# The six projections of half the tokens, issued over four steps of cross-attention instead of three

## The chip, the cores and the metric

The kernel runs on one core of a Trainium2 chip. The metric is the device time of one execution in microseconds (us): median 1030.58 of three runs, 1029.69 to 1031.92.

The engines are named as the profile names them: PE is TensorE (matmuls and transposes), PEld its weight load, DVE is VectorE, ACT is ScalarE, POOL is GpSimd, SP is the queue that issues most DMAs. They run side by side, each in its own order of instructions, and wait for one another through semaphores.

## What is computed

One decoder layer on 8 sequences of 128 tokens, 512 wide, in 32-bit floats: self-attention, cross-attention with a context of the same size, and a feed-forward part, each on a layer norm of its input and added to it. The change lies in the cross-attention alone:

```python
q = (query @ Wq).reshape(nb, q_len, H, D).transpose(0, 2, 1, 3)     # H = 32 heads, D = 128
k = (key @ Wk).reshape(nb, q_len, KVH, D).transpose(0, 2, 1, 3)     # KVH = 8
v = (value @ Wv).reshape(nb, q_len, KVH, D).transpose(0, 2, 1, 3)
q = q * cos + _rotate_half(q) * sin
k = k * cos + _rotate_half(k) * sin
...
scores = jnp.einsum('bhqd,bhkd->bhqk', q, k) / jnp.sqrt(jnp.float32(D))
scores = jnp.where(mask == 0, jnp.float32(-1000000000.0), scores)
attn = jax.nn.softmax(scores, axis=-1)
x = jnp.einsum('bhqk,bhkd->bhqd', attn, v)
x = x.transpose(0, 2, 1, 3).reshape(nb, q_len, H * D)
return x @ Wo
```

## The kernel before

Cross-attention runs over 8 groups `g`; a group is one key head with its four query heads. A group has 8 steps `b`, one for each sequence. Step `b` issues on PE, in this order:

- the scores of sequence `b` (line 1030, four small matmuls into SC, bank 2 or 3);
- projections and output products, as two tables say. `blocks_in(b)` lists projections as (piece `j`, half of the tokens, group ahead). Pieces are 0 = keys, 1 to 4 = the four query heads, 5 = values; they are called K, q0, q1, q2, q3 and V below. Each is 12 matmuls (line 624, called by `project`) into PB, bank 0 for even `j` and bank 1 for odd `j`. Steps 0 to 3 serve half 1 of this group, steps 4 to 7 half 0 of the next. `outputs_in(b)` lists output products O(y), also 12 matmuls of line 624, all into YB, bank 7: O(-3), O(-2), O(-1) (sequences 5 to 7 of the group before) in steps 0, 1 and 2, none in step 3, O(0) in step 4, O(1) and O(2) in step 5, O(3) in step 6, O(4) in step 7. The order in a step is: first projection, outputs named `before`, second projection, outputs named `after`;
- the product of probabilities and values of sequence `b - 2` (called pv here, three matmuls of line 624 into OB, bank 6);
- the transposes of the probabilities of sequence `b - 1` (line 1060, into TB, bank 4 or 5);
- in the step that has V, four transposes of the values (`transpose_v`, line 998).

The other engines follow the same steps. For each piece but V, DVE applies the rotation with three operations (`rope`, lines 838 to 840) and POOL adds the two parts (`rope_sum`, line 798). V goes another way: ACT copies the projected bank to SBUF (`v_copy`, line 919, tile `rotated`), PE transposes it back into the same bank, ACT and DVE take high and low part (`v_high`, line 925; `v_low`, line 844). In a step DVE first masks the scores (line 873) and takes their negated maximum (line 876), then comes to the ropes and the additions of outputs to `x` (`add_output`, line 852), then to the reciprocal of the row sums (line 895) and two low parts (lines 898, 901). ACT first takes the four exponentials of the step (line 938), then `v_copy` where the step has V, then two copies (lines 948, 953), `v_high`, and casts of weights (line 610), whose low parts POOL takes (line 618). POOL in a step comes to the rope sums, then to the normalisation of the probabilities (line 813), then to the weights.

Three waits matter to what follows. All output products share one bank, so each one waits for the addition of the one before it (this is the wait on `x2`); the transposes of the values wait for `v_copy`, which stands behind the step's exponentials:

```python
    pe.wait_ge(sem["x2"], SEQS * g + y)          # in output(g, y)
    pe.wait_ge(sem["vT"], 2 * g + half + 1)      # in transpose_v(g, half)
    pe.wait_ge(sem["probsT_low"], n - 1)         # ahead of the pv product
```

The first group has no outputs in its steps 0 to 2; the last one has no projections in steps 4 to 7 and orders its outputs differently from step 5 on.

Of the kernel before, what the change touches and what calls it, by code (L numbers as in the profile page):

```python
# [581 lines left out]
PIECES = 6  # L582
# [51 lines left out]
def norm_stats(nc, dve, m, sem, k):  # L634
    if k >= EARLY:
        dve.wait_ge(sem["x2"], SEQS * (GROUPS - 1) + NORM_SEQ[k] + 1)
    if k > 0:
        dve.wait_ge(sem["norm_mv"], k)
    nc.vector.bn_stats(m["norm_stats"][:], m["x"][:, NORM_SEQ[k], :]).then_inc(sem["norm_stats"], 1)  # L639
    dve.wait_ge(sem["norm_stats"], k + 1)  # L640
    nc.vector.bn_aggr(m["norm_mv"][:, k, :], m["norm_stats"][:]).then_inc(sem["norm_mv"], 1)  # L641
# [57 lines left out]
def half_of(t, half):  # L699
    return t[..., half * HT:(half + 1) * HT]  # L700


def cross_attention(nc, m, sem, ps, io):
# [7 lines left out]
    with ExitStack() as stack:  # L711
# [18 lines left out]
        def norm_bank(k):  # L730

            return PB[k % 2] if k >= EARLY else (SC[1], YB)[k]

        def rows_of(k):
            return m["norm_rows"][:, k % 2, :] if k >= EARLY else last_hs[:, k, :]
# [6 lines left out]
        def norms_in(table, b, last, tail):  # L742
            return table.get(SEQS + b if tail else b, []) if last else []

        def blocks_in(b):

            pairs = {0: (0, 1), 1: (2, 3), 2: (4, 5)}
            return [(j, 1, 0) for j in pairs.get(b, ())] + [(j, 0, 1) for j in pairs.get(b - 4, ())]

        def turns_in(b, last):  # L750
# [23 lines left out]
        @block.sync  # L774
        def _(sp):
            def body(g, last):
                for b in range(SEQS):
                    for which, ahead, t in turns_in(b, last):
                        if which < PIECES:
                            source = piece_source(io, which, g + 1)  # L780
                        else:
                            source = io["wo2"][bass.ds((g * QUAD + which - PIECES) * P, P), :]
                        load_piece(sp, m, sem, PIECES + TURNS * g + t, (PIECES + t) % SLOTS, source)

            with sp.Fori(0, GROUPS - 1) as g:
                body(g, False)
            body(GROUPS - 1, True)
            sp.wait_ge(sem["piece_split"], PIECES + TURNS * (GROUPS - 1) + QUAD)
            load_ff_rows(sp, m, sem, io, 0)
# [37 lines left out]
        @block.vector  # L827
        def _(dve):
            def rope(g, half, j, first=False):

                rr = 10 * g + 5 * half + j
                pb = PB[j % 2]
                dve.wait_ge(sem["projected"], 12 * g + 6 * half + j + 1)
                if not first and j == 0:
                    dve.wait_ge(sem["v_transposed"], 2 * g + half)
                if not first or j >= 2:
                    dve.wait_ge(sem["roped"], rr - 1)
                nc.vector.tensor_tensor(rot[:, (half + j) % 2, :], pb[:], half_of(m["cosT"][:], half), ALU.mult)  # L838
                nc.vector.tensor_tensor(cross[0:64, (half + j) % 2, :], pb[64:128, :], half_of(m["sinT"][0:64, :], half), ALU.mult)
                nc.vector.tensor_tensor(cross[64:128, (half + j) % 2, :], pb[0:64, :], half_of(m["sinT"][64:128, :], half), ALU.mult).then_inc(sem["rope_read"], 1)  # L840

            def v_low(g, half):
                dve.wait_ge(sem["v_high"], 2 * g + half + 1)
                nc.vector.tensor_tensor(v[:, 1, half * HALF:(half + 1) * HALF, :], PB[1][:].rearrange("p (b d) -> p b d", b=HALF),
                                        v[:, 0, half * HALF:(half + 1) * HALF, :].bitcast(F32), ALU.subtract).then_inc(sem["v_low"], 1)

            def add_output(g, y, first):

                dve.wait_ge(sem["out2"], SEQS * g + y + 1)
                if not (first and y == 0):  # L850
                    dve.wait_ge(sem["x2"], SEQS * g + y)
                nc.vector.tensor_tensor(x[:, y % SEQS, :], x[:, y % SEQS, :], YB[:], ALU.add).then_inc(sem["x2"], 1)  # L852

            for k in range(EARLY):
                norm_stats(nc, dve, m, sem, k)
            for k in range(EARLY):
                norm_rows(nc, dve, m, sem, k, rows_of(k))
            for j in range(PIECES - 1):
                rope(0, 0, j, first=True)
                if j < EARLY:  # L860
                    norm_low(nc, dve, m, sem, j, norm_bank(j))
            v_low(0, 0)

            def body(g, first, last, tail=False):
                for b in range(3 if tail else SEQS):
                    n = SEQS * g + b
                    blocks = [x for x in blocks_in(b) if not (x[2] and last)] if not tail else []
                    if not tail:

                        dve.wait_ge(sem["scores2"], n + 1)  # L870
                        if not first or b >= 2:
                            dve.wait_ge(sem["probs_transposed2"], n - 1)
                        nc.vector.scalar_tensor_tensor(out=S[:, b % 2], in0=SC[b % 2][:].rearrange("p (h k) -> p h k", h=QUAD), scalar=SCALE2,
                                                       in1=cap[:, b, :].unsqueeze(1).to_broadcast([P, QUAD, P]), op0=ALU.mult, op1=ALU.min).then_inc(sem["masked2"], 1)
                        dve.wait_ge(sem["masked2"], n + 1)
                        nc.vector.tensor_reduce(negmax[:, b % 2, :], S[:, b % 2], AX.X, ALU.max, negate=True).then_inc(sem["max2"], 1)  # L876
                    for j, half, ahead in blocks[:1]:
                        rope(g + ahead, half, j)
                    before, after, late = outputs_in(b, first, last, tail)
                    for y in before:  # L880
                        add_output(g, y, first)
                    for j, half, ahead in blocks[1:]:
                        if j < PIECES - 1:
                            rope(g + ahead, half, j)
                    for y in after:
                        add_output(g, y, first)
                    for k in norms_in(NORM_LOWS, b, last, tail):
                        norm_low(nc, dve, m, sem, k, norm_bank(k))
                    for k in norms_in(NORM_STATS, b, last, tail):
                        norm_stats(nc, dve, m, sem, k)  # L890
                    for k in norms_in(NORM_ROWS, b, last, tail):
                        norm_rows(nc, dve, m, sem, k, rows_of(k))
                    if not tail:
                        dve.wait_ge(sem["exp2"], n + 1)
                        nc.vector.reciprocal(rinv[:, b % 2, :], rowsum[:, b % 2, :]).then_inc(sem["rinv2"], 1)  # L895
                    if (not first or b >= 2) and (not tail or b < 2):
                        dve.wait_ge(sem["outT_high"], n - 1)
                        nc.vector.tensor_tensor(oT[:, b % 2, 1], OB[:], oT[:, b % 2, 0].bitcast(F32), ALU.subtract).then_inc(sem["outT_low"], 1)  # L898
                    if (not first or b >= 1) and (not tail or b < 1):
                        dve.wait_ge(sem["probsT_high"], n)  # L900
                        nc.vector.tensor_tensor(PT[:, 1], TB[(b - 1) % 2][:], PT[:, 0].bitcast(F32), ALU.subtract).then_inc(sem["probsT_low"], 1)
                    for j, half, ahead in blocks[1:]:
                        if j == PIECES - 1:
                            v_low(g + ahead, half)
                    for y in late:
                        add_output(g, y, first)

            body(0, True, False)
            with dve.Fori(1, GROUPS - 1) as g:
                body(g, False, False)  # L910
            body(GROUPS - 1, False, True)
            body(GROUPS, False, True, tail=True)

# [63 lines left out]
        def _(pe):  # L977
# [42 lines left out]
            def body(g, first, last, tail=False):  # L1020
                for b in range(3 if tail else SEQS):
                    n = SEQS * g + b
                    blocks = [x for x in blocks_in(b) if not (x[2] and last)] if not tail else []
# [30 lines left out]
                    if (not first or b >= 1) and (not tail or b < 1):  # L1054
# [4 lines left out]
                        for h in range(QUAD):  # L1059
                            i = nc.tensor.transpose(TB[(b - 1) % 2][:, h * P:(h + 1) * P], S[:, (b - 1) % 2, h, :], ident[:])  # L1060
                        i.then_inc(sem["probs_transposed2"], 1)
                    for j, half, ahead in blocks[1:]:
                        if j == PIECES - 1:
                            transpose_v(g + ahead, half)
                    for y in late:
# [300 lines left out]
```

## Time and profile before

| what | value |
|---|---|
| time, median of three runs | 1030.58 us (1029.69 to 1031.92) |
| profiled execution: span from first to last instruction | 1029.7 us |
| PE busy (matmuls) | 1003.1 us, 97% |
| DVE busy | 581.3 us, 56% |
| ACT busy | 428.1 us, 42% |
| POOL busy | 381.6 us, 37% |
| mean granted TensorE clock over the span | 0.992 of full |

No time of its own is shown for the profiled execution beside its span; the span is 0.9 us below the median of the runs. The cross-attention fills the stretch from about 236 to 828 us. Matmuls overlap, so the start of one row to the start of the next is what a row takes of PE's time, and the busy time of a row is a little more than that.

### The profile page before, as it was taken

Reading aid. Unit: us, or ns where it says so; the run is one execution under the profiler, and the core shown is the slowest. Engines: PE = TensorE matmul, PEld = TensorE weight load, DVE = VectorE, ACT = ScalarE, POOL = GpSimd, SP = SyncE. Lnnn points to the kernel's source line nnn. Section 1 sums busy time; section 2 is a strip of 40 time slices with the busy share of each in tenths; the row PEclk is TensorE's granted clock in tenths of the full one; section 3 lists DMA queues with packets and bytes.
Section 4 is the critical chain, followed back from the end, with each engine's and each line's share of the span. In section 5 each row is a group of like instructions: output and inputs, shape, how many; then the busy total and the mean of one; then the engine's idle time right before and its main releaser. Section 6 shows DMA issues by size and latency. Waiting matters only on the chain. (4 is left out here: it accounts for less than half of the span.)

```text
span 1029.7 us, 16071 instructions
## 1 busy us (share of the span) xinstructions
PE 1003.1 (97%) x5260; PEld 822.9 (80%) x5260; DVE 581.3 (56%) x973; ACT 428.1 (42%) x1239; POOL 381.6 (37%) x375
## 2 busy tenths in 40 slices
PE   5999999989999999999999999999999999999998
PEld 3787777876888888888888888888887778888787
DVE  3765555636776666767666666766765852222101
ACT  2777666751533433533533434434334433332100
POOL 7422222253642642643634534626424222222100
PEclk8999999989999999999999999999999999999999
DMA  6000000211110210210210201201100022221001
GB/s 199 12 11 11 11 10 10 62 52 52 50 54 1 73 32 0 71 31 0 74 27 20 72 10 31 61 10 49 43 1 32 1 62 61 61 69 47 11 31 41
DMA packets 45699, 39.98 MB, mean 39 GB/s; under 512 B 3617, under 2 KB 34465, under 8 KB 45665
## 3 DMA queue, kind: packets, MB, share of 16 engines
q1 hardware_dynamic: 45280, 38.48, 12.7%
q0 software_dynamic: 384, 1.05, 0.3%
q8 instruction: 20, 0.33, 0.1%
q14 instruction: 15, 0.11, 0.0%
HBM read 37.43 MB, written 2.10 MB: 38 GB/s over the span
## 5 line engine op out<-in xcount | busy, mean ns | idle before, releaser
L624 PE MATMUL bank<-cross_wo_hl,cross_outT_hl 128*128 128x512 f32 x768 | 191.7, 398 | 1.0 <-POOL cross_wo_hl L618 0.6
L624 PE MATMUL bank<-hsT_hl,cross_wqkv_hl 128*128 128x512 f32 x768 | 188.2, 394 | 0.0
L624 PEld LDWEIGHTS bank<-cross_wo_hl,cross_outT_hl 128*128 128x128 f32 x768 | 143.1, 188 | 35.5 <-POOL cross_wo_hl L618 1.6
L624 PEld LDWEIGHTS bank<-hsT_hl,cross_wqkv_hl 128*128 128x128 f32 x768 | 141.9, 188 | 29.3
L938 ACT ACTIVATE cross_scores<-cross_scores,cross_negmax 128x128 f32<-128x128 f32 x256 | 99.8, 391 | 127.1 <-DVE cross_negmax L876 127.1
L798 POOL TENSOR_TENSOR cross_qT<-rotated,rotated_other_half 128x512 f32<-128x512 f32 x64 | 82.8, 1293 | 162.0 <-DVE rotated_other_half L840 162.0
L624 PE MATMUL bank<-hsT_hl,ff_gate_upT_hl 128*128 128x512 f32 (+1 forms) x528 | 126.3, 395 | 0.5 <-DVE ff_gate_upT_hl L1140 0.5
L624 PEld LDWEIGHTS bank<-hsT_hl,ff_gate_upT_hl 128*128 128x128 f32 (+1 forms) x528 | 96.3, 186 | 21.9 <-DVE ff_gate_upT_hl L1140 0.8
L948 ACT CAST cross_outT_hl<-bank 128x512 fp32r<-128x512 f32 x64 | 37.1, 579 | 143.4 <-PE bank L624 142.5
L838 DVE TENSOR_TENSOR rotated<-bank,cosT 128x512 f32<-128x512 f32 x80 | 55.2, 690 | 71.4 <-PE bank L624 71.2
L624 PE MATMUL bank<-ctxT_hl,cross_wqkv_hl 128*128 128x512 f32 x384 | 94.3, 394 | 1.1 <-PEq L74 1.1
L813 POOL TENSOR_TENSOR cross_scores<-cross_scores,cross_rinv 128x512 f32<-128x512 f32 x64 | 66.6, 1041 | 67.1 <-DVE cross_rinv L895 65.8
L399 ACT ACTIVATE self_probs<-self_scores,self_negmax 128x128 f32<-128x128 f32 x256 | 81.8, 393 | 20.8 <-DVE self_negmax L293 20.8
L624 PEld LDWEIGHTS bank<-ctxT_hl,cross_wqkv_hl 128*128 128x128 f32 x384 | 71.0, 188 | 16.4 <-issue 1.9
L898 DVE TENSOR_TENSOR cross_outT_hl<-bank,cross_outT_hl 128x512 fp32r<-128x512 f32 x64 | 43.5, 679 | 56.3 <-ACT cross_outT_hl L948 56.3
L290 DVE TENSOR_TENSOR self_scores<-bank,alibi_bias 128x512 f32<-128x512 f32 x64 | 44.0, 688 | 44.9 <-PE bank L498 44.5
L1127 POOL TENSOR_TENSOR ff_hT_hl<-ff_work,ff_hT_hl 128x512 f32 (+2 forms) x22 | 28.4, 1292 | 107.1 <-ACT ff_hT_hl L1202 107.1
L1030 PE MATMUL bank<-cross_kT,cross_qT 128*128 128x128 f32 x512 | 67.6, 275 | 0.0
L518 PEld LDWEIGHTS bank<-self_v_and_ones,self_probsT 128*128 128x128 f32 x512 | 63.8, 196 | 2.7 <-ACT self_probsT L384 2.6
L518 PE MATMUL bank<-self_v_and_ones,self_probsT 128*128 (+1 forms) x512 | 63.5, 257 | 2.2 <-ACT self_probsT L384 2.2
L852 DVE TENSOR_TENSOR x<-x,bank 128x512 f32<-128x512 f32 x64 | 44.0, 687 | 34.9 <-PE bank L624 34.7
L1030 PEld LDWEIGHTS bank<-cross_kT,cross_qT 128*128 128x128 f32 x512 | 62.4, 192 | 0.2
(121 smaller groups left out, 1565.7 us busy)
## 6 DMA issues: line engine op xcount, KB each, us to landing
staged_rows<-in_wq SPq DMA_DIRECT2D x32, 256.0 KB, 2.8
staged_rows<-in_wo SPq DMA_DIRECT2D x32, 256.0 KB, 2.7
staged_rows<-in_wg SPq DMA_DIRECT2D x10, 256.0 KB, 2.6
staged_rows<-in_wu SPq DMA_DIRECT2D x10, 256.0 KB, 2.8
staged_rows<-in_wd SPq DMA_DIRECT2D x10, 256.0 KB, 3.0
ctx_tok<-in_ctx SPq DMA_DIRECT2D x8, 256.0 KB, 2.6
staged_rows<-in_wk SPq DMA_DIRECT2D x8, 256.0 KB, 3.1
staged_rows<-in_wv SPq DMA_DIRECT2D x8, 256.0 KB, 3.1
```

The source lines that it names most:

```text
L290: nc.vector.tensor_tensor(S[:, s % 2], SC[s % 2][:].rearrange("p (h k) -> p h k", h=QUAD), bias[:, QUAD * s:QUAD * s + QUAD, :], ALU.add). ...
L399: e = nc.scalar.activation(PR[:, s % 2, j, :], S[:, s % 2, j, :], ACT.Exp, bias=negmax[:, s % 2, j:j + 1])
L518: i = nc.tensor.matmul(OB[r // HALF][:, c:c + HD1 + 1], PT[:, r % 2, j, :], v[:, bass.ds(owner, 1), :].rearrange("p b d -> p (b d)"), star ...
L624: i = nc.tensor.matmul(out, stationary[:, a], moving[:, b], start=(first and k == 0), stop=(last and k == 2))
L798: nc.gpsimd.tensor_tensor(half_of(dst, half), rot[:, (half + j) % 2, :], cross[:, (half + j) % 2, :], ALU.add).then_inc(sem["roped"], 1)
L813: nc.gpsimd.tensor_tensor(S[:, b % 2], S[:, b % 2], rinv[:, b % 2, :].unsqueeze(2).to_broadcast([P, QUAD, P]), ALU.mult).then_inc(sem["pro ...
L838: nc.vector.tensor_tensor(rot[:, (half + j) % 2, :], pb[:], half_of(m["cosT"][:], half), ALU.mult)
L852: nc.vector.tensor_tensor(x[:, y % SEQS, :], x[:, y % SEQS, :], YB[:], ALU.add).then_inc(sem["x2"], 1)
L898: nc.vector.tensor_tensor(oT[:, b % 2, 1], OB[:], oT[:, b % 2, 0].bitcast(F32), ALU.subtract).then_inc(sem["outT_low"], 1)
L938: e = nc.scalar.activation(S[:, b % 2, h, :], S[:, b % 2, h, :], ACT.Exp, bias=negmax[:, b % 2, h:h + 1], accum_out=rowsum[:, b % 2, h:h + 1])
L948: nc.scalar.copy(oT[:, b % 2, 0], OB[:]).then_inc(sem["outT_high"], 1)
L1030: i = nc.tensor.matmul(SC[b % 2][:, h * P:(h + 1) * P], qT[:, h, b * P:(b + 1) * P], kT[:, b * P:(b + 1) * P], start=True, stop=True)
```

## The change

The table of projections is spread over four steps instead of three. V stands alone in step 3 (and 7), q1 alone in step 1 (and 5), q2 and q3 in step 2 (and 6). The other edits let a step whose only projection is V go through `v_low` and `transpose_v` and not through `rope`; ACT and POOL read the same table.

```diff
-            pairs = {0: (0, 1), 1: (2, 3), 2: (4, 5)}
+            pairs = {0: (0, 1), 1: (2,), 2: (3, 4), 3: (5,)}
             return [(j, 1, 0) for j in pairs.get(b, ())] + [(j, 0, 1) for j in pairs.get(b - 4, ())]
...
                     for j, half, ahead in blocks[:1]:
-                        rope(g + ahead, half, j)
+                        if j < PIECES - 1:
+                            rope(g + ahead, half, j)
...
-                    for j, half, ahead in blocks[1:]:
+                    for j, half, ahead in blocks:
                         if j == PIECES - 1:
                             v_low(g + ahead, half)
...
-                    for j, half, ahead in blocks[1:]:
+                    for j, half, ahead in blocks:
                         if j == PIECES - 1:
                             transpose_v(g + ahead, half)
```

PE, end of step 2, step 3 and start of step 4 of a middle group, before. The products from `ctxT_hl` are V (bank 1) and K (bank 0) of this place, bank 6 is pv, line 1060 transposes probabilities, line 998 the values, line 1030 makes scores:

```order
L624 MATMUL bank1<-ctxT_hl,cross_wqkv_hl 128x512 x12
L624 MATMUL bank6<-cross_probsT_hl,cross_v_hl 128x512 x3
L1056 REGISTER_ALU
L1060 MATMUL bank5<-ident,cross_scores 128x128 x4
L996 REGISTER_ALU
L998 MATMUL bank1<-ident,rotated 128x128 x4
L1030 MATMUL bank3<-cross_kT,cross_qT 128x128 x4
L624 MATMUL bank6<-cross_probsT_hl,cross_v_hl 128x512 x3
L1056 REGISTER_ALU
L1060 MATMUL bank4<-ident,cross_scores 128x128 x4
L1026 REGISTER_ALU
L1030 MATMUL bank2<-cross_kT,cross_qT 128x128 x4
```

The same place of the changed kernel, whose lines here are one higher:

```order
L624 MATMUL bank0<-hsT_hl,cross_wqkv_hl 128x512 x12
L624 MATMUL bank6<-cross_probsT_hl,cross_v_hl 128x512 x3
L1057 REGISTER_ALU
L1061 MATMUL bank5<-ident,cross_scores 128x128 x4
L1031 MATMUL bank3<-cross_kT,cross_qT 128x128 x4
L987 REGISTER_ALU
L624 MATMUL bank1<-ctxT_hl,cross_wqkv_hl 128x512 x12
L624 MATMUL bank6<-cross_probsT_hl,cross_v_hl 128x512 x3
L1057 REGISTER_ALU
L1061 MATMUL bank4<-ident,cross_scores 128x128 x4
L997 REGISTER_ALU
L999 MATMUL bank1<-ident,rotated 128x128 x4
```

V has moved from step 2 into step 3, between the scores and the pv product; its transposes come at the end of step 3; step 2 now ends with q3 from `hsT_hl`.

ACT, step 2 of a middle group, before (line 938 are the exponentials, line 919 is `v_copy`, lines 948 and 953 the two copies, line 925 `v_high`):

```order
L938 ACTIVATE cross_scores,cross_rowsum<-cross_scores,cross_negmax 128x128 x4
L917 REGISTER_ALU
L918 ISA
L919 COPY rotated<-bank1 128x512
L948 CAST cross_outT_hl<-bank6 128x512
L953 CAST cross_probsT_hl<-bank5 128x512
L925 CAST cross_v_hl<-bank1 128x512
```

ACT, step 3 of a middle group, after:

```order
L939 ACTIVATE cross_scores,cross_rowsum<-cross_scores,cross_negmax 128x128 x4
L918 REGISTER_ALU
L919 ISA
L920 COPY rotated<-bank1 128x512
L949 CAST cross_outT_hl<-bank6 128x512
L954 CAST cross_probsT_hl<-bank4 128x512
L926 CAST cross_v_hl<-bank1 128x512
```

The copy of V keeps its place behind the exponentials of its step, but that is now step 3.

PE, step 5 of a middle group, before, from the scores to pv (bank 7 holds the output products, banks 0 and 1 the projections q1 and q2):

```order
L1030 MATMUL bank3<-cross_kT,cross_qT 128x128 x4
L986 REGISTER_ALU
L624 MATMUL bank0<-hsT_hl,cross_wqkv_hl 128x512 x12
L624 MATMUL bank7<-cross_wo_hl,cross_outT_hl 128x512 x12
L986 REGISTER_ALU
L989 REGISTER_ALU
L624 MATMUL bank1<-hsT_hl,cross_wqkv_hl 128x512 x12
L624 MATMUL bank7<-cross_wo_hl,cross_outT_hl 128x512 x12
L624 MATMUL bank6<-cross_probsT_hl,cross_v_hl 128x512 x3
```

And after:

```order
L1031 MATMUL bank3<-cross_kT,cross_qT 128x128 x4
L987 REGISTER_ALU
L624 MATMUL bank0<-hsT_hl,cross_wqkv_hl 128x512 x12
L624 MATMUL bank7<-cross_wo_hl,cross_outT_hl 128x512 x24
L624 MATMUL bank6<-cross_probsT_hl,cross_v_hl 128x512 x3
```

q2 has left step 5 for step 6; O(1) and O(2) stand side by side, both in bank 7.

## Rows read from the trace of the kernel before

**Rows 1.** The page: busy time, share of the span, instructions.

```profile
PE 1003.1 (97%) x5260; PEld 822.9 (80%) x5260; DVE 581.3 (56%) x973; ACT 428.1 (42%) x1239; POOL 381.6 (37%) x375
```

**Rows 2.** PE's waits: for whom, us in total, times, longest.

```profile
PE bank L624 <- DVE cross_probsT_hl L901: 2.2, 9, 0.3
```

**Rows 3.** Timeline of PE, middle group, step 1's products to step 4: start, length.

```profile
411.70 1.06 PE L1030 MATMUL bank<-cross_kT,cross_qT 128*128 128x128 f32 x8
412.51 3.01 PE L624 MATMUL bank<-hsT_hl,cross_wqkv_hl 128*128 128x512 f32 x12
415.36 2.97 PE L624 MATMUL bank<-cross_wo_hl,cross_outT_hl 128*128 128x512 f32 x12
418.17 2.89 PE L624 MATMUL bank<-ctxT_hl,cross_wqkv_hl 128*128 128x512 f32 x12
420.90 0.86 PE L624 MATMUL bank<-cross_probsT_hl,cross_v_hl 128*128 128x512 f32 x3
421.60 0.60 PE L1060 MATMUL bank<-ident,cross_scores 128*128 128x128 f32 x4
422.03 0.60 PE L998 MATMUL bank<-ident,rotated 128*128 128x128 f32 x4
422.47 1.06 PE L1030 MATMUL bank<-cross_kT,cross_qT 128*128 128x128 f32 x8
423.76 0.97 PE L624 MATMUL bank<-cross_probsT_hl,cross_v_hl 128*128 128x512 f32 x3 [0.23 <-DVE cross_probsT_hl L901]
424.57 0.60 PE L1060 MATMUL bank<-ident,cross_scores 128*128 128x128 f32 x4
425.00 1.06 PE L1030 MATMUL bank<-cross_kT,cross_qT 128*128 128x128 f32 x8
```

**Rows 4.** Timeline of the same group, one group on: the same scores.

```profile
498.01 1.06 PE L1030 MATMUL bank<-cross_kT,cross_qT 128*128 128x128 f32 x8
```

**Rows 5.** Timeline of DVE and ACT around the scores of 411.70.

```profile
410.85 0.69 DVE L838 TENSOR_TENSOR rotated<-bank,cosT 128x512 f32<-128x512 f32 x1 [2.13 <-PE bank L624]
414.25 0.68 DVE L873 SCALAR_TENSOR_TENSOR cross_scores<-bank,cap 128x512 f32<-128x512 f32 x1
414.29 1.03 POOL L813 TENSOR_TENSOR cross_scores<-cross_scores,cross_rinv 128x512 f32<-128x512 f32 x1
415.68 0.40 ACT L938 ACTIVATE cross_scores<-cross_scores,cross_negmax 128x128 f32<-128x128 f32 x1 [1.51 <-DVE cross_negmax L876]
417.15 0.18 ACT L938 ACTIVATION_READ_ACCUMULATOR cross_scores<-cross_scores,cross_negmax 128x1 f32 x1
```

**Rows 6.** Timeline of the opening of cross-attention: copy and transposes of V.

```profile
253.94 0.58 ACT L919 COPY rotated<-bank 128x512 f32<-128x512 f32 x1 [10.32 <-PE bank L624]
254.58 0.66 PE L998 MATMUL bank<-ident,rotated 128*128 128x128 f32 x4 [0.68 <-ACT rotated L919]
255.07 1.06 PE L1030 MATMUL bank<-cross_kT,cross_qT 128*128 128x128 f32 x8
```

**Rows 7.** Timeline of DVE: the addition of the output product of 415.36.

```profile
418.37 0.69 DVE L852 TENSOR_TENSOR x<-x,bank 128x512 f32<-128x512 f32 x1 [0.63 <-PE bank L624]
```

**Rows 8.** Timeline of the first group: scores of step 1, POOL's probabilities of step 0.

```profile
261.44 1.05 PE L1030 MATMUL bank<-cross_kT,cross_qT 128*128 128x128 f32 x8
265.06 1.03 POOL L813 TENSOR_TENSOR cross_scores<-cross_scores,cross_rinv 128x512 f32<-128x512 f32 x1
```

**Rows 9.** Timeline of the last group, step 4: weights on POOL, O(0) and pv.

```profile
789.01 5.02 POOL L618 TENSOR_TENSOR cross_wo_hl<-staged_rows,cross_wo_hl 128x512 fp32r<-128x512 f32 x4 [3.69 <-ACT cross_wo_hl L610]
790.88 1.70 PE L624 MATMUL bank<-cross_wo_hl,cross_outT_hl 128*128 128x512 f32 x6
794.89 0.86 PE L624 MATMUL bank<-cross_probsT_hl,cross_v_hl 128*128 128x512 f32 x3
```

**Rows 10.** Stretches: length, then busy time (instructions) of the engines, granted clock, DMA.

```profile
216.00:220.00 4.00, 2.78 (x13) 1.54 (x12) 1.99 (x5) 0.76 (x3) 4.00 (x4) 1.00 0.34 98
224.00:228.00 4.00, 3.10 (x15) 3.02 (x16) 0.68 (x2) 0.00 (x0) 0.00 (x0) 0.50 0.00 0
824.00:828.00 4.00, 3.11 (x13) 2.18 (x12) 1.46 (x3) 0.58 (x1) 0.00 (x0) 1.00 0.00 0
```

## The prediction

> **What bounds the kernel now.** I read the page first: PE is busy for 1003.1 of 1029.7 us [rows 1]; no other engine comes near. A busy figure says little by itself, since matmuls overlap, so next I read PE's waits and its timeline. In the whole of cross-attention PE hardly waits: the longest entry that repeats is pv waiting for `probsT_low`, 9 times, 2.2 us in all [rows 2]. The timeline shows the rest as a closed chain, each row starting where the one before lets it [rows 3]. So in this stage PE's own order sets the time: a thing that shortens nothing on PE and removes no wait gains nothing, and a wait put into PE's order is lost at full length, as nothing behind it has slack to give back. A group takes 498.01 - 425.00 = 73.01 us [rows 3, 4].
>
> Costs on PE from start to start [rows 3]: scores 0.81, a projection right behind scores 2.85, an output product behind a projection 2.81, a product behind an output 2.73, pv 0.70, transposes of probabilities 0.43, transposes of values 0.44.
>
> **What the change removes.** No instruction of weight goes or comes; V, q1, q2, q3 change places. Step 3 now has only scores, pv and transposes, and pv waits there for its input: from the scores (422.47) to the transposes (424.57) it takes 2.10 us where 0.81 + 0.70 = 1.51 would do [rows 3]. With V between, 2.85 us longer, this input is in time. Gain 0.59 us a group. Against it, one more projection stands right behind scores: 2.85 instead of 2.73, loss 0.12.
>
> **First new wait, step 3: the transposes of V.** They wait for `v_copy`, and ACT does that behind the four exponentials of the same step. Before, V was the second projection of step 2, and the exponentials of step 2 were long over when it ended. Now V ends 0.81 + 2.85 us behind the start of the step's scores, and the question is when the exponentials of step 3 end. The trace has the same situation on the other engines, one step earlier: the step behind one with projection, output, projection with a rope. Step 2 of the changed kernel has just that shape (q2, O(-1), q3), with the same work for DVE, as step 1 of the kernel before, whose last product is followed by the scores of 411.70. I take t = 411.70 as zero. DVE can begin the rope of the last projection only at 410.85, and behind it come reciprocal and two low parts, so it masks the new scores at 414.25 (2.55 us after t), ACT begins its exponentials at 415.68, and the last read ends at 417.33, 5.63 us after t [rows 5]. `v_copy` takes 0.58, and PE starts its transposes 0.06 after its end [rows 6]: 5.63 + 0.58 + 0.06 = 6.27 us after t, with 0.02 of hand-over 6.29. PE itself would be there after 0.81 + 2.85 + 0.70 + 0.43 = 4.79 us. The new wait is 1.50 us. Behind it the transposes take 0.49 instead of 0.44 [rows 6], 0.05 more. I see no cover: what stands behind on PE is scores, K, O(0), all in order. Bounds: if DVE were free as soon as scores are there (0.8 to 0.9 us after t instead of 2.55), the wait would be gone (1.50 - 1.7 < 0); but its work is bound to the end of q3 by the same rows, so I hold the low end at 1.2. The high end is 1.9, if ACT's three weight casts, which stand before these exponentials, end late.
>
> The half of the next group has the same in step 7, but there O(4) stands behind V: PE comes to the transposes 4.79 + 2.81 = 7.60 us after the scores, later than 6.29. No wait. What else waits in step 3: the transposes of step 2's probabilities, at 0.81 + 2.85 + 0.70 = 4.36 us, want POOL's product, which in the analogous row ends at 415.32, 3.62 after t [rows 5]: in time by 0.7 us. ACT's copies and DVE's low parts behind `v_copy` come later by some 3 us; they are wanted by pv of step 4 and q0 of step 4, which start over 7 us behind step 4's scores. Covered.
>
> **Second new wait, step 5: O(2) behind O(1).** All outputs are made in bank 7, and O(2) may start only when DVE has added O(1) to `x`. Before, q2 stood between. The addition for an output product that starts at 415.36 runs from 418.37 to 419.06 [rows 7], so with 0.06 to PE the next output could start at 419.12, and the next product in order started at 418.17 [rows 3]: 0.95 us of wait. A product that starts after a gap costs about 0.1 more (2.85 against 2.73 behind scores, above, is the nearest pair). 1.05 us in each of the groups 0 to 6; the last group has an order of its own there. Bounds: nothing less than the addition itself (0.69) and, if DVE were still at q1's rope when O(1) ends, 1.5. The rope of this place ends some 0.6 us before (the idle time shown ahead of the addition, 0.63), so I stay with 1.05.
>
> By the Trainium skill, page "PSUM — Partial Sum Buffer", section "PSUM bank collisions raise a hardware error", two engines must not touch one bank at a time and a semaphore has to guard it; by that rule, too, no part of the addition can run under O(2), and the trace has no output product that starts inside an addition.
>
> **First and last group.** In the first group there are no outputs in steps 0 to 2, so with q2 gone from step 1 the transposes of step 0's probabilities come 0.81 + 2.85 us behind the scores of 261.44, at 265.10; POOL ends its product at 266.09 [rows 8]. With 0.1 of hand-over and 0.05 behind it: 1.15 us, once. In the last group, O(0) stands right behind the scores of step 4 and waits for weights from POOL: it takes 794.89 - 790.88 = 4.01 us instead of 2.88 (2.81 and some 0.07 behind scores) [rows 9]. The change makes step 3 longer by over 4 us while the casts begin earlier (`v_copy` and `v_high` no longer stand before them), so POOL is done in time: by its 5.02 us for four, begun 3.6 us after the scores of step 3, it ends at 8.6; the scores of step 4 now start 6.29 + 0.49 = 6.78 after those of step 3, and the fourth quarter of O(0) is wanted 0.81 + 2.16 later, near 9.7. Gain 1.13, once. Weights of the projections: q2 of the next half is now wanted a step later, q3 not sooner, so no DMA or piece comes late. The DMAs keep their order and turns.
>
> **The sum.** A group from 1 to 6: -0.59 + 0.12 + 1.50 + 0.05 + 1.05 = +2.13. Six of them: +12.8. First: 2.13 + 1.15 = +3.3. Last: -0.59 + 0.12 + 1.55 - 1.13 = -0.05. In all +16.0 us: the profiled span 1029.7 becomes 1045.7, and the median, 0.9 above the span, 1030.58 + 16.0 = 1046.6 us. That is 1.6% slower. With the low ends of both waits (1.2 and 0.7) it is 8 x 0.3 + 7 x 0.35 = 4.9 less, 1041.7; with the high ends (1.9 and 1.5) 8 x 0.4 + 7 x 0.45 = 6.4 more, 1053.0; both at an end together is unlikely.
>
> **Rivals.**
> - *Faster: V fills the hole and nothing else happens.* Then -0.59 + 0.12 a group, 8 x 0.47 = 3.8, and 1.1 of the last group: 1025.7 us. It needs the exponentials of step 3 to end by 4.1 us after the scores and the addition to cost nothing. For it: step 3 is the only place where PE waits now. Against it: 5.63 in the rows, and one bank for O. Chance 3%.
> - *Only the wait of step 3.* DVE adds early or O(2) is not held: 1046.6 - 7 x 1.05 = 1039.2. Chance 4%.
> - *Only the wait of step 5.* DVE catches up: 1046.6 - 8 x 1.55 = 1034.2. Chance 4%.
> - *The clock falls as well.* Ahead of the cross-attention the granted clock stood at 1.2 GHz (0.50) in 224 to 228 us, behind a stretch with PE busy for 2.78 of 4 us; but with 3.11 of 4 us busy at 824 it stayed at 2.4 GHz (1.00) [rows 10]. Around the new wait of 1.5 us PE is busy for about 2.5 of 4 us at worst and fully again behind it. One fall like that one, some 8 us at half speed, costs about 4 us: once or twice gives 1051 to 1055, in every group 1046.6 + 32 = 1079. Chance 8%. The Trainium skill, page "TensorE: Matmul & The Clock Gate", section "A second HAM failure mode: psum-queue depth-cycling", tells of a kernel whose short pauses between groups of matmuls over PSUM banks made the clock go up and down; by that rule this change, which adds such pauses, would end with this rival. The rows before show none of it with pauses of 0.23 us.
>
> The forecast itself has 81%. No case that I see ends within 0.2% of before (2.1 us, about what a measurement of this kernel can tell from no change); 1% for what I have not seen. Faster 3%, same 2%, slower 95%. The range, 1042.0 to 1051.5, takes the forecast with one wait at an end of its bounds and one fall of the clock, and leaves out the two rivals with a single wait.
>
> **What would show it.** In a middle group: PE's transposes of values in step 3 with a wait of near 1.5 us put down to ACT's copy (some 10 to 12 us in all over 8 groups, since the shown idle time is less than the loss by some tenths); O(2) in step 5 with a wait of 0.7 to 0.8 us put down to DVE's addition, 7 times; no wait for `probsT_low` in step 3; a group of 75.1 us instead of 73.0; step 7 without a wait; clock 1.00 throughout. I am wrong if a group's time stays at 73 or less, if the exponentials of step 3 begin earlier than 3.9 us after its scores, or if a third wait stands in PE's list, for POOL in step 3 above all, where the margin is 0.7 us.

## The result and the profile after

The changed kernel takes 1045.64 us (median of four runs, 1044.74 to 1046.67) against 1030.47 us for the kernel before (four runs), a ratio of 1.0148 with a 95% interval of 1.0134 to 1.0162. It is slower by 15.2 us; the forecast was 16.0.

The page of the changed kernel, the same line as [rows 1]:

```profile
PE 1002.3 (96%) x5260; PEld 820.5 (79%) x5260; DVE 581.3 (56%) x973; ACT 427.3 (41%) x1239; POOL 381.1 (37%) x375
```

The work is the same, with the same count of instructions. PE's list of waits (us in total, times, longest) is what changed:

```profile
PE bank L999 <- ACT rotated L920: 10.1, 9, 1.2
PE bank L624 <- DVE x L852: 6.5, 8, 0.9
...
PE bank L1061 <- POOL cross_scores L813: 0.9, 1, 0.9
...
PE bank L624 <- DVE cross_probsT_hl L902: 0.3, 1, 0.3
```

The wait for `probsT_low` of [rows 2] has gone from 9 times to once. In its place the transposes of V wait for ACT's copy (8 groups, and the opening as before), O(2) waits for the addition (7 groups, and once in the tail as before), and the opening group waits once for POOL. The timeline of PE in a middle group, the answer to [rows 3], from pv of step 2 to the scores of step 4, and the scores of the next group, the answer to [rows 4]:

```profile
421.32 0.86 PE L624 MATMUL bank<-cross_probsT_hl,cross_v_hl 128*128 128x512 f32 x3
...
422.46 1.06 PE L1031 MATMUL bank<-cross_kT,cross_qT 128*128 128x128 f32 x8
423.27 3.00 PE L624 MATMUL bank<-ctxT_hl,cross_wqkv_hl 128*128 128x512 f32 x12
426.11 0.86 PE L624 MATMUL bank<-cross_probsT_hl,cross_v_hl 128*128 128x512 f32 x3
426.81 0.60 PE L1061 MATMUL bank<-ident,cross_scores 128*128 128x128 f32 x4
428.61 0.66 PE L999 MATMUL bank<-ident,rotated 128*128 128x128 f32 x4 [1.21 <-ACT rotated L920]
429.11 1.06 PE L1031 MATMUL bank<-cross_kT,cross_qT 128*128 128x128 f32 x8
...
504.22 1.06 PE L1031 MATMUL bank<-cross_kT,cross_qT 128*128 128x128 f32 x8
```

pv of step 3 (426.11) follows V without a gap, so the wait for `probsT_low` is gone there. The transposes of V start 1.80 us behind those of the probabilities, where 0.43 would do: 1.37 us lost (the shown idle time, 1.21, is less than the loss, since the ends of matmuls are modelled). A group takes 504.22 - 429.11 = 75.11 us instead of 73.01. Step 5 of the same group:

```profile
440.25 3.01 PE L624 MATMUL bank<-hsT_hl,cross_wqkv_hl 128*128 128x512 f32 x12
443.10 2.97 PE L624 MATMUL bank<-cross_wo_hl,cross_outT_hl 128*128 128x512 f32 x12
446.94 3.04 PE L624 MATMUL bank<-cross_wo_hl,cross_outT_hl 128*128 128x512 f32 x12 [0.87 <-DVE x L852]
449.82 0.86 PE L624 MATMUL bank<-cross_probsT_hl,cross_v_hl 128*128 128x512 f32 x3
```

From O(1) to O(2) it takes 3.84 us, where an output product otherwise takes 2.81. What the other engines do at both places, the answer to [rows 5, 7]:

```profile
421.61 0.69 DVE L838 TENSOR_TENSOR rotated<-bank,cosT 128x512 f32<-128x512 f32 x1 [2.13 <-PE bank L624]
425.00 0.68 DVE L873 SCALAR_TENSOR_TENSOR cross_scores<-bank,cap 128x512 f32<-128x512 f32 x1
425.04 1.03 POOL L813 TENSOR_TENSOR cross_scores<-cross_scores,cross_rinv 128x512 f32<-128x512 f32 x1
426.44 0.40 ACT L939 ACTIVATE cross_scores<-cross_scores,cross_negmax 128x128 f32<-128x128 f32 x1 [1.58 <-DVE cross_negmax L876]
...
427.90 0.19 ACT L939 ACTIVATION_READ_ACCUMULATOR cross_scores<-cross_scores,cross_negmax 128x1 f32 x1
427.99 0.56 ACT L920 COPY rotated<-bank 128x512 f32<-128x512 f32 x1
...
446.11 0.69 DVE L852 TENSOR_TENSOR x<-x,bank 128x512 f32<-128x512 f32 x1 [0.51 <-PE bank L624]
```

The mask stands 2.54 us behind the scores (2.55 was forecast), the exponentials 3.98 (3.98), and `v_copy` comes right behind them. V lay finished in its bank from 426.27 on (start 423.27 and 3.00 long), 1.7 us before ACT read it.

The span grew by 13.2 us only, the median by 15.2. The difference of the two does not come from the change. PE's rows at both ends of cross-attention, first scores and first transposes of the feed-forward part, are these in the changed kernel, and the last one of the kernel before (its first scores stand in [rows 6]):

```profile
253.24 1.06 PE L1031 MATMUL bank<-cross_kT,cross_qT 128*128 128x128 f32 x8
...
841.81 1.06 PE L1220 MATMUL bank<-ident,staged_rows 128*128 128x128 f32 x8 [1.05 <-PEq L711]
```

```profile
828.59 1.06 PE L1219 MATMUL bank<-ident,staged_rows 128*128 128x128 f32 x8 [1.05 <-PEq L711]
```

The stretch grew from 828.59 - 255.07 to 841.81 - 253.24, by 15.05 us. The profiled execution of the changed kernel came to cross-attention 1.83 us earlier, as the last section shows.

### The profile page after: what moved, and what is told of

Same layout as the page of the kernel before. It is cut to its first block and busy times, and to the rows that moved or that the text cites. A ratio compares the mean times of both kernels' runs of the same rounds, so it can differ in the third digit from the quotient of the medians.

```text
span 1042.9 us, 16071 instructions
## 1 busy us (share of the span) xinstructions
PE 1002.3 (96%) x5260; PEld 820.5 (79%) x5260; DVE 581.3 (56%) x973; ACT 427.3 (41%) x1239; POOL 381.1 (37%) x375
## 3 DMA queue, kind: packets, MB, share of 16 engines
q0 software_dynamic: 384, 1.05, 0.3%
## 5 line engine op out<-in xcount | busy, mean ns | idle before, releaser
L618 POOL TENSOR_TENSOR cross_wqkv_hl<-staged_rows,cross_wqkv_hl 128x512 fp32r<-128x512 f32 x48 | 61.0, 1295 | 6.7 <-ACT cross_wqkv_hl L610 6.6
```

Of the source, the lines that this page charges most:

```text
L618: nc.gpsimd.tensor_tensor(dst[:, 1], src, dst[:, 0].bitcast(F32), ALU.subtract).then_inc(sem["piece_split"], 1)
```

## The experiments

Each is the changed kernel with the edit shown or described. "Group" is the time from the scores of step 4 to those of the next group's step 4, in the middle of the kernel; steps 3 and 5 are the times from scores to scores.

| kernel | step 3 | step 5 | group | median us | ratio to before (95%) |
|---|---|---|---|---|---|
| before | 2.53 | 13.14 | 73.01 | 1030.47 | 1 |
| the change | 6.65 | 11.52 | 75.11 | 1045.64 | 1.0148 (1.0134 to 1.0162) |
| v_copy first | 5.22 | 11.52 | 73.68 | 1034.49 | 1.0044 (1.0027 to 1.0061) |
| v_copy in the middle | 5.88 | 11.52 | 74.33 | 1039.67 | 1.0094 (1.0077 to 1.0110) |
| O(1) first | 6.65 | 10.40 | 73.97 | 1036.54 | 1.0057 (1.0040 to 1.0074) |
| both orders | 5.22 | 10.41 | 72.55 | 1026.52 | 0.9964 (0.9950 to 0.9978) |
| V alone | 5.70 | 13.14 | 73.04 | 1029.81 | 0.9992 (0.9982 to 1.0001) |
| q2 alone | 2.53 | 11.52 | 74.09 | 1039.38 | 1.0083 (1.0068 to 1.0099) |
| both orders, opening group | 5.22 | 10.40 | 72.55 | 1026.91 | 0.9967 (0.9955 to 0.9979) |
| V alone, v_copy first | 5.22 | 13.14 | 72.56 | 1026.47 | 0.9966 (0.9953 to 0.9978) |

The medians of the kernel before lay between 1029.65 and 1030.54 in the three sets of runs; the ratios compare the runs within a set, and may differ by 0.1% from the quotient of two medians of this table.

**v_copy first.** ACT copies V ahead of its exponentials, and ahead of its wait for their input:

```diff
-                        act.wait_ge(sem["max2"], n + 1)
+                        values = [(g + ahead, half) for j, half, ahead in blocks_in(b) if j == PIECES - 1 and not (ahead and last)]
                         for h in range(QUAD):
+                            if h == 0:
+                                for which in values:
+                                    v_copy(*which)
+                            if h == 0:
+                                act.wait_ge(sem["max2"], n + 1)
...
                         e.then_inc(sem["exp2"], 1)
-                        for j, half, ahead in blocks_in(b):
-                            if j == PIECES - 1 and not (ahead and last):
-                                v_copy(g + ahead, half)
```

> The changed kernel, with ACT's copy of V (v_copy) ahead of the four exponentials of its step instead of behind them, all else as changed. My theory (the wait of step 3 is v_copy queued behind exponentials that can't start before 4 us after the scores): V ends 3.8 us after the scores, the copy ends at 4.4, PE comes at 4.8, so the wait put down to ACT's copy goes but for the opening one (10.1 us in all to 0.7). A middle group falls from 75.11 to 73.7 us, the time from 1045.6 to about 1034.3 us. The exponentials of step 3 start some 0.45 us later, which nothing on PE should feel. Rival (DVE's late chain behind q3's rope is itself what PE needs, so a wait on the probabilities or on a low part takes the place): the group stays at 74.5 or above and another wait of near 1 us stands in step 3 or 4; time above 1040.

Measured: 1034.49 us, a group 73.68. Timeline of step 3, PE and ACT:

```profile
423.40 0.86 PE L624 MATMUL bank<-cross_probsT_hl,cross_v_hl 128*128 128x512 f32 x3
423.68 0.59 ACT L920 COPY rotated<-bank 128x512 f32<-128x512 f32 x1 [1.54 <-PE bank L624]
424.10 0.60 PE L1063 MATMUL bank<-ident,cross_scores 128*128 128x128 f32 x4
424.54 0.60 PE L1001 MATMUL bank<-ident,rotated 128*128 128x128 f32 x4
424.97 1.06 PE L1033 MATMUL bank<-cross_kT,cross_qT 128*128 128x128 f32 x8
```

The copy now waits for PE, runs under pv, and PE goes through in steps of 0.70, 0.44 and 0.43. Nothing took the wait's place in the following steps: step 3 fell by 1.43, the group by 1.43. The loss of step 3 is the place of `v_copy` in ACT's order.

**v_copy in the middle.** The same, with the copy behind two of the four exponentials: the first `if h == 0` reads `if h == 2`.

> The changed kernel, with v_copy behind two of the four exponentials. My theory: two exponentials end about 4.85 us after the scores, the copy 0.58 later, PE starts its transposes near 5.5 instead of 6.15, so the loss of step 3 is 0.7 us instead of 1.4; a group 74.45, the time about 1040.1 us. Rival (it matters only whether DVE has begun the step's chain, not how many exponentials stand ahead): the loss is either whole (1045.6) or gone (1034.3).

Measured: 1039.67 us. PE's wait for the copy, in total, times, longest:

```profile
PE bank L1001 <- ACT rotated L920: 4.0, 9, 0.7
```

Step 3 takes 5.88: the loss goes with the number of exponentials ahead of the copy, 0, 2 and 4 giving 5.22, 5.88 and 6.65. The rival, all or nothing, is ruled out.

**O(1) first.** Step 5 in the order O(1), q1, O(2), on PE and on DVE alike (shown for PE):

```diff
+                    before, after, late = outputs_in(b, first, last, tail)
+                    if b == 5:
+                        for y in before:
+                            output(g, y, first, last)
                     for j, half, ahead in blocks[:1]:
                         project(g + ahead, half, j)
-                    before, after, late = outputs_in(b, first, last, tail)
-                    for y in before:
-                        output(g, y, first, last)
+                    if b != 5:
+                        for y in before:
+                            output(g, y, first, last)
```

> The changed kernel, with step 5 in the order O(1), q1, O(2) instead of q1, O(1), O(2), on PE and on DVE, all else as changed. My theory (O(2) waits for the addition of O(1) out of the one bank): a projection between them hides the addition, the wait put down to DVE's line 852 falls from 8 times (6.5 us) to the one of the tail (0.4), a group from 75.11 to 74.1, the time from 1045.6 to about 1038.4 us. Rival (a second product of outputs is slow for another reason, its input oT or DVE's load): the group stays within 0.3 us of 75.1 and the time within 2 us of 1045.6.

Measured: 1036.54 us, a group 73.97. Timeline of step 5 on PE:

```profile
438.93 3.05 PE L624 MATMUL bank<-cross_wo_hl,cross_outT_hl 128*128 128x512 f32 x12
441.81 2.92 PE L624 MATMUL bank<-hsT_hl,cross_wqkv_hl 128*128 128x512 f32 x12
444.57 2.97 PE L624 MATMUL bank<-cross_wo_hl,cross_outT_hl 128*128 128x512 f32 x12
```

Same products, no gap: 2.88, 2.76, then 2.81 to pv (447.38). The addition of O(1) runs under q1, as DVE's row shows:

```profile
442.01 0.69 DVE L852 TENSOR_TENSOR x<-x,bank 128x512 f32<-128x512 f32 x1
```

Step 5 falls by 1.12 and the group by 1.14. The time is 1.9 us below the 1038.4 expected. The kernel before was 0.8 us lower in this set of runs than in the first (1029.65 against 1030.47); the other 1.1 us is within the interval of the ratio, 0.17% to either side.

**Both orders.** The two edits together.

> Both edits together: v_copy ahead of the exponentials, and O(1), q1, O(2) in step 5. My theory: the two losses are independent and PE's order is the bound, so the gains add: 11.3 + 7.2 us off 1045.6, about 1027.1 us, a group 72.65, 3.4 us below the kernel before (1030.5). Rival (with both waits gone a third engine or chain binds, DVE or POOL at the start of step 3 above all): a group at 73.0 or more, time 1030 or more.

Measured: 1026.52 us, a group 72.55. The losses add up: 75.11 - 1.43 - 1.14 = 72.54. In the middle groups no other engine binds with both gone, and this kernel beats the kernel before by 0.36% (0.22 to 0.50).

**V alone.** The table is `{0: (0, 1), 1: (2, 3), 2: (4,), 3: (5,)}`, ACT in the order of the change.

> One part of the change alone: only V moves, to step 3 and 7; q1 and q2 stay together in step 1 and 5 (table 0: K q0, 1: q1 q2, 2: q3, 3: V), ACT in the order of the change. My theory (how long PE waits for v_copy depends on when DVE gets to the scores of step 3, which hangs on the last rope of step 2): step 2 is now one projection and one output, as step 1 of the changed kernel, after which the exponentials begin 3.1 us after the scores instead of 3.98. So v_copy ends near 5.3 and PE loses 0.6 us instead of 1.4; step 3 takes 5.85 instead of 6.65, a group 73.2 us, and with the last group's gain the time is within 1 us of the kernel before (1029.7). Rival (the loss of step 3 is the same wherever q3 stands, as it is four exponentials in any case): step 3 takes 6.65, a group 74.0, the time 1036. No wait of PE for the addition in step 5 in either case.

Measured: 1029.81 us, ratio 0.9992 (0.9982 to 1.0001), no change that can be told. Timeline of DVE, ACT and PE at the end of step 2 and in step 3, whose scores start 5.70 us before those of step 4, at 419.93:

```profile
417.70 0.68 DVE L840 TENSOR_TENSOR rotated_other_half<-bank,sinT 64x512 f32<-64x512 f32 x1
...
421.53 0.68 DVE L873 SCALAR_TENSOR_TENSOR cross_scores<-bank,cap 128x512 f32<-128x512 f32 x1
...
422.97 0.40 ACT L939 ACTIVATE cross_scores<-cross_scores,cross_negmax 128x128 f32<-128x128 f32 x1 [0.63 <-DVE cross_negmax L876]
...
424.52 0.56 ACT L920 COPY rotated<-bank 128x512 f32<-128x512 f32 x1
...
425.14 0.66 PE L999 MATMUL bank<-ident,rotated 128*128 128x128 f32 x4 [0.25 <-ACT rotated L920]
425.63 1.06 PE L1031 MATMUL bank<-cross_kT,cross_qT 128*128 128x128 f32 x8
```

The mask stands 1.60 us behind the scores instead of 2.54, the exponentials 3.04 instead of 3.98, and PE loses 0.42 instead of 1.37. So the same four exponentials cost a third as much when step 2 ends with an output and not with a projection that DVE must rotate first. DVE's last row for q3 ends at 418.38 here, 1.55 us ahead of the scores of step 3; in the change DVE begins q3 at 421.61, when PE has made it, and ends three rows of about 0.7 us later, behind those scores (422.46). That is the other half of the cause. What holds the mask in this kernel is the addition of O(-1) and the low parts behind it (from 419.01 on).

**q2 alone.** The table is `{0: (0, 1), 1: (2,), 2: (3, 4, 5)}`; V stays in step 2.

> The other part alone: q2 moves to step 2 and 6, V stays there with q3 (table 0: K q0, 1: q1, 2: q2 q3 V). My theory: only the wait of O(2) for the addition of O(1) comes, 1.1 us in seven groups, and the opening group's wait for POOL's probabilities, near 1 us; step 3 stays at 2.53 with its wait for probsT_low. A group 74.1 us, the time 1038.2 against 1029.7 of the kernel before. Rival (three products behind one output make step 3's wait longer, since DVE comes later): step 3 above 2.8 us and a group above 74.4.

Measured: 1039.38 us. Two of PE's waits in cross-attention, the one for the addition as in the change and the one for `probsT_low` as before:

```profile
PE bank L624 <- DVE x L852: 6.5, 8, 0.9
...
PE bank L624 <- DVE cross_probsT_hl L902: 2.2, 9, 0.3
```

The opening group's wait for POOL is there too (0.9 us shown, once). Step 3 stays at 2.53, step 5 has the 11.52 of the change. Against before the two parts give +1.08 (q2) and +0.03 (V) a group, 1.11 together, where the change gives 2.10: the parts are not independent, since V alone leaves q3 in another place of step 2, and so shortens the wait for the copy. With that difference in step 3, 6.65 - 5.70 = 0.95, the sum is 2.06.

**Both orders, opening group.** The opening group keeps q2 in step 1 and moves V alone there.

> Both orders, and in the opening group alone q2 stays in step 1 (0: K q0, 1: q1 q2, 2: q3, 3: V there). My theory: the opening group's transposes of step 1 no longer wait for POOL (0.9 us shown, near 1.0 lost), all else as with both orders: group 72.55, time 1025.5 us, 0.4% below the kernel before. Rival (the wait moves on within the opening group): no gain over 1026.5.

Measured: 1026.91 us, where 1025.5 was expected; the ratio 0.9967 against 0.9964 is no gain. Timelines of PE and POOL of the opening group:

```profile
274.39 0.86 PE L624 MATMUL bank<-cross_probsT_hl,cross_v_hl 128*128 128x512 f32 x3
276.20 0.65 PE L1073 MATMUL bank<-ident,cross_scores 128*128 128x128 f32 x4 [0.94 <-POOL cross_scores L815]
...
270.11 3.80 POOL L618 TENSOR_TENSOR cross_wqkv_hl<-staged_rows,cross_wqkv_hl 128x512 fp32r<-128x512 f32 x3
273.86 1.29 POOL L800 TENSOR_TENSOR cross_qT<-rotated,rotated_other_half 128x512 f32<-128x512 f32 x1
275.11 1.04 POOL L815 TENSOR_TENSOR cross_scores<-cross_scores,cross_rinv 128x512 f32<-128x512 f32 x1
```

The rival was right: the wait has moved on from step 1 to step 3. There POOL works without a gap on three pieces of weights, a rope sum and the probabilities that PE wants. From its first scores to those of step 4 the opening group takes 24.37 us, and 24.31 with both orders. That this group is the tight one because its steps 0 to 2 have no output products (its step 2 takes 4.80 us here) fits the rows, but no run tests it.

**V alone, v_copy first.** The table of "V alone" with the first edit of ACT.

> Only V moves (0: K q0, 1: q1 q2, 2: q3, 3: V), and v_copy stands ahead of the exponentials; step 5 as in the kernel before (q1, O(1), q2, O(2)). My theory: PE's order is the bound and any order without a wait gives the same sum, so a group takes 72.6 us and the time is 1025.5 us, as with both orders and the opening group mended. Rival (two projections more in steps 1 and 5 leave DVE and POOL late for step 3 or 7): a wait on PE's list that the kernel with both orders has not, group 72.9 or more, time above 1028.

Measured: 1026.47 us, ratio 0.9966 (0.9953 to 0.9978), a group 72.56: against both orders (72.55) no difference. These two orders of the same products, both without a wait in the middle groups, take the same time; this one needs the smaller edit. The expectation, 1025.5, was for an opening group without a wait, but this kernel has one for POOL too, in step 3 (1.0 us, once).

## Why the prediction was right

- **PE's order is the bound and hands every wait on at full length**: shown. Taking the waits away one at a time moved the group by 1.43 and 1.14 us, about what they had cost (1.37 and 1.03, and a slower start of the product behind each), both together by the sum, and two different orders without them take the same time (72.55 and 72.56).
- **Gain of step 3** (0.59 less 0.12): both orders and V alone with v_copy first give 72.55 and 72.56, 0.46 and 0.45 below before; forecast 0.47.
- **First new wait, 1.50 forecast**: 1.37 measured. The chain was right row by row (mask 2.54 for 2.55, exponentials 3.98 for 3.98). What was off is its end, by 0.14 in all (6.15 us after the scores for 6.29): I let the copy start behind the last read of the accumulator, 5.63 us after the scores; it started at 5.53, while that read still ran until 5.63; the copy took 0.56 for 0.58, and the 0.02 of hand-over did not show. The experiments with v_copy show the place in ACT's order as the cause, V alone shows DVE's rope as the other half, as the prediction put it.
- **No wait in step 7**: right, PE's list has one wait for the copy per group, and the opening one.
- **Second new wait, 1.05 forecast**: 1.12 measured (11.52 against 10.40 without it). The mechanism was right, the size a little low. The addition started 0.04 us behind the modelled end of O(1) and took 0.69 as forecast, but PE started 0.14 after its end, where I had taken 0.06.
- **The opening group's wait for POOL**: there, 0.93 shown and 1.11 lost with the slower start behind it (264.81 - 260.41 - 2.85 - 0.44); forecast 1.15. My price of that group was too high all the same, by a misread base. I charged it with step 3 as in a middle group (2.53 before), but it took more, as these rows of PE of the kernel before show, from scores to scores 2.80:

```profile
276.18 1.06 PE L1030 MATMUL bank<-cross_kT,cross_qT 128*128 128x128 f32 x8
277.47 0.97 PE L624 MATMUL bank<-cross_probsT_hl,cross_v_hl 128*128 128x512 f32 x3 [0.23 <-DVE cross_probsT_hl L901]
...
278.98 1.06 PE L1030 MATMUL bank<-cross_kT,cross_qT 128*128 128x128 f32 x8
```

- **The last group's O(0)**, gain 1.13 forecast: 808.34 - 805.45 = 2.89 us instead of 4.01 [rows 9], 1.12. The cover was as forecast, POOL's weights done before they were wanted:

```profile
801.57 5.00 POOL L618 TENSOR_TENSOR cross_wo_hl<-staged_rows,cross_wo_hl 128x512 fp32r<-128x512 f32 x4
...
805.45 3.05 PE L624 MATMUL bank<-cross_wo_hl,cross_outT_hl 128*128 128x512 f32 x12
808.34 0.86 PE L624 MATMUL bank<-cross_probsT_hl,cross_v_hl 128*128 128x512 f32 x3
```

- **The sum**: 16.0 forecast, 15.05 on PE's timeline of cross-attention: 14.67 for the seven stretches from step 4 to step 4 (14.91 forecast), +1.73 for the opening up to its step 4 (2.23 forecast), -1.35 from the last step 4 on (-1.13 forecast). In the seven stretches the first wait came out 0.12 lower a group (1.43 with the slower transposes, for 1.55) and the second 0.08 higher (1.12 to 1.14 for 1.05): these two errors nearly cancel, and that is luck. The opening's 0.50 is the misread base (0.27) and its step 3, 6.56 us where 6.78 was charged (0.22). The last group's 0.22 lies in its step 5, 7.62 us for 7.88 before, which the forecast left as it was: the output product behind the transposes starts 0.35 us behind them (813.86 to 814.21) and not 0.61 (800.40 to 801.01), since DVE ends the addition that it waits for at 814.05, and before, 0.32 us behind the end of the product and not 0.04, at 800.87.
- **The chances** add up to 101% (81 + 8 + 4 + 4 + 3, and 1 for what was not seen), a slip that moves nothing else.
- **Rivals**: the clock did not fall in cross-attention (granted 1.00 in the changed kernel's stretches from 240 to 845 us), so pauses of 1.4 us once and 1.0 us once in 75 us do not bring it down here. No kernel with more or longer pauses was run. That rival, for which the Trainium skill's page "TensorE: Matmul & The Clock Gate" speaks in its section on psum-queue depth-cycling, did not happen in any of the nine kernels. The two rivals with a single wait were built in effect (v_copy first, O(1) first) and gave 1034.5 and 1036.5; forecast for them were 1034.2 and 1039.2. The second is 2.7 us off: one part is the forecast's own 1.0 too much, another the kernel before, 0.8 us lower in that set of runs.

## What to carry to other kernels

Where one engine runs without gaps, moving equal work along its order changed the time here by the waits that it made or took away, and by little else (0.12 us for a product behind scores); so list, for each moved piece, what stands right behind it in the same bank and what must be done with it on the other engines before its next reader. A helper's place in the order of another engine (a copy behind four exponentials) is safe only as long as the producer comes late; when the producer moves to the front of a step, its consumer has to move as well. Here V moved with its copy saves 0.34%, and V moved alone gives nothing. With q2 moved as well, out of the place between two products of one bank, where it had covered the addition, the change costs 1.5%.

## What the runs showed of the hardware that I had not expected

The same instructions ahead of cross-attention differ by up to 1.8 us between executions. Stretches of the kernel before, and then of the changed one (length, busy time and count of PE, PEld, DVE, ACT and POOL, then granted clock, DMA share, GB/s):

```profile
20.00:24.00 4.00, 2.32 (x9) 1.59 (x8) 3.50 (x7) 1.46 (x5) 3.60 (x6) 0.56 0.00 0
24.00:28.00 4.00, 4.00 (x11) 2.27 (x9) 2.81 (x6) 3.38 (x10) 3.52 (x8) 0.59 0.00 0
```

```profile
20.00:24.00 4.00, 1.84 (x9) 1.36 (x10) 2.86 (x6) 1.28 (x5) 3.60 (x7) 1.00 0.00 0
24.00:28.00 4.00, 4.00 (x23) 2.77 (x21) 3.90 (x8) 3.56 (x11) 3.52 (x7) 1.00 0.00 0
```

In the first the granted clock was at 1.2 GHz for most of these 8 us, in the second at 2.4 GHz throughout. What PE did ahead of it was nearly the same in both: a wait until 6.3 and 6.1 us for DVE's line 237, one of 1.5 and 1.7 us for the DMA of `self_wq`, some 8 us of work, and then waits of 0.77 us for ACT and 1.15 for POOL. Behind these the clock fell in the one and not in the other. At PE's next transposes (line 433) the kernel before was 0.64 us ahead (22.69 against 23.33), at its wait for `ctxT_hl` (line 459) it was 1.55 us behind (40.01 against 38.46), and at the transposes of V ahead of cross-attention 1.83 us (254.58 against 252.75). None of the edited code runs there.

The ten profiled executions fall into two kinds. In five the clock was low in these stretches (the kernel before, O(1) first, both orders, V alone, q2 alone), and the first scores came at 254.21 to 255.07; in the other five it was not, and they came at 252.76 to 253.28. The first five have a mean clock of 0.991 or 0.992 over the span, the others 0.995. The kernel before shows both kinds: of its 17 runs in the last set, the four with 0.995 took 1029.36 to 1029.76 us, the thirteen with 0.992 took 1029.92 to 1031.85. What decides it stays open. It is about half as large as the gains told above (some 3.5 us), which is why the groups' times were read beside the medians.

For the forecast's rival of the clock this means that a fall can come behind pauses of about 1 us; it did so ahead of cross-attention only, and in none of the ten executions within it.
